# Edge features and their weight in two 12-bit halves: a pass through DRAM in layer 1's stage, and attention's edge product as two one-pass products

## What is computed

```python
# layer 1: three times, the mean over each node's incoming edges
x = segment_sum(x[src], dst) / max(counts, 1)

# layer 3: GATv2 attention, 8 heads, with 32 features on each edge
ea = concatenate([edge_attr, edge_attr.mean(0) for each node's own loop])
x_l, x_r, e = x @ W_l, x @ W_r, ea @ W_e
m = leaky_relu(x_l[src] + x_r[dst] + e, 0.2)
alpha = einsum('ehc,hc->eh', m, att)         # then softmax over each node's incoming edges
out = segment_sum(x_l[src] * a, dst)
```

## Time and profile before

| | us |
|---|---|
| median of 3 runs | 2247.66 (2246.16 to 2248.53) |
| profiled execution, first to last instruction | 2246.0 |
| PE busy in it | 1815.0 |
| DVE busy | 1330.2 |
| ACT busy | 1054.8 |
| POOL busy | 845.9 |

### The profile page before, as it was taken

One profiled execution on the slowest core, in us unless ns is written; L12 is line 12 of the kernel. 1 busy time (PEld: TensorE's weight loads), 2 busy tenths in 40 slices (PEclk: granted clock), 3 DMA queues, 4 the chain that ended last, 5 costly groups with the idle time before them and its releaser, 6 DMA issues. The chain is left out here.

```text
span 2246.0 us, 35303 instructions
## 1 busy us (share of the span) xinstructions
PE 1815.0 (81%) x10709; PEld 1262.9 (56%) x10709; DVE 1330.2 (59%) x3119; ACT 1054.8 (47%) x2333; POOL 845.9 (38%) x886
## 2 busy tenths in 40 slices
PE   5677799979999983678887888878878878888876
PEld 2567765557888851345554555545545555555554
DVE  6999967674333353755555555555545555554585
ACT  0689877645423451144434444444434344444465
POOL 1000000010000015766666666666666666666500
PEclk9555589999999997889898989998898889998887
DMA  3100000014400012323332333333322223332311
GB/s 91 40 2 1 2 8 0 0 29 124 118 1 5 3 34 74 85 75 85 80 82 75 85 81 78 82 82 83 81 78 81 81 78 85 82 80 78 79 34 29
DMA packets 132486, 133.22 MB, mean 59 GB/s; under 512 B 29049, under 2 KB 102354, under 8 KB 132306
## 3 DMA queue, kind: packets, MB, share of 16 engines
q1 hardware_dynamic: 104530, 73.76, 11.5%
q0 software_dynamic: 27776, 57.20, 10.3%
HBM read 126.05 MB, written 4.82 MB: 58 GB/s over the span
## 5 line engine op out<-in xcount | busy, mean ns | idle before, releaser
L2198 POOL DMA_INDIRECT rows<-x_l,src x856 | 821.0, 959 | 467.7 <-issue 224.7
L2323 ACT ACTIVATE bent<-psum 128x512 f32<-128x512 f32 x214 | 126.9, 594 | 532.0 <-remote 323.3
L2216 PE MATMUL psum<-hot,x_r_parts 128*128 128x256 bf16 x1284 | 205.8, 296 | 183.6 <-DVE hot L2377 97.1
L2284 PE MATMUL psum<-both,node_hot 128*128 128x144 f32 x1712 | 300.4, 318 | 56.0 <-issue 43.4
L2284 PEld LDWEIGHTS psum<-both,node_hot 128*128 128x128 f32 x1712 | 262.1, 211 | 130.3 <-issue 116.4
L2216 PEld LDWEIGHTS psum<-hot,x_r_parts 128*128 x1284 | 131.0, 102 | 342.9 <-issue 320.1
L2381 DVE TENSOR_TENSOR bent<-psum,bent 128x512 f32<-128x512 f32 x214 | 147.0, 687 | 218.8 <-ACT bent L2323 130.4
L2338 ACT ACTIVATE apart<-iota,rel 128x128 bf16<-128x128 f32 x856 | 270.5, 388 | 0.4 <-PE psum L2284 0.4
L2219 PE MATMUL psum<-edges,w_e 128*128 128x512 f32 x428 | 252.1, 671 | 10.3 <-issue 10.0
L2471 DVE TENSOR_TENSOR acc<-acc,psum 128x144 f32 x428 | 127.5, 298 | 224.1 <-remote 163.8
L2236 PE MATMUL psum<-bent,att_heads 128*128 128x512 f32 x428 | 232.0, 633 | 2.9 <-issue 1.7
(11 more groups left out here) (344 smaller groups left out, 2395.9 us busy)
## 6 DMA issues: line engine op xcount, KB each, us to landing
rel_row<-e_rel_rows SPq DMA_DIRECT2D x107, 256.0 KB
edges<-edge_t SPq DMA_DIRECT2D x428, 32.0 KB
rows<-x_l,src POOLq DMA_INDIRECT x856
edge_part<-edge_t SPq DMA_DIRECT2D x40, 320.0 KB, 3.1
new<-e_new_before SPq DMA_DIRECT2D x26, 64.0 KB
new<-e_new_behind SPq DMA_DIRECT2D x26, 64.0 KB
ht<-x SPq DMA_DIRECT2D x6, 256.0 KB, 2.8
x_l<-rows SPq DMA_DIRECT2D x4, 320.0 KB
```

Source lines behind the costliest of these rows:

```text
L2198: e.indirect_dma_start(rows[:, g % ring, j * ROW:(j + 1) * ROW], None, k.xl, bass.IndirectOffsetOnAxis(ap=src[:, at:at + 1], axis=0)).then ...
L2216: e.matmul(z[:, half], row_parts.parts[:, bass.ds(blocks[j], 1), q, :].rearrange("p o f -> p (o f)"), hot[:, two, half], start=j + q == 0, ...
L2284: final = e.matmul(to, near_hot[:, at, j, :], both[:, at, j, :], start=j % 2 == 0, stop=j % 2 == 1)
```

## The change

The edge features and `W_e` are each split into an upper half, which is the number rounded to the type `float32r`, and a lower half, which is the rest; the sum of the two is exact. A `float32r` operand goes through TensorE in one pass.

**In layer 1's stage** ACT's copy writes the upper half to a place of its own (the tile `hs`, which layer 1's last slots need later), POOL subtracts it from the piece, and SP stores both to two new DRAM tables, `edge_upper` and `edge_lower`. Pieces are 2 quads instead of 5, so there are 101 instead of 41, in 5 buffers (`edge_part`) and 4 (upper halves). ACT sums three pieces in each of the slots 0 to 33.

**In attention** SP loads four pieces in place of two for each group, the upper halves into rows 0 to 31 and the lower ones into rows 32 to 63 of `edges`. `w_e` has two matrices, each with the same half of the weight in both row ranges, so two products give all four combinations of halves.

```diff
-    share = -(-s.quads // (2 * s.nb))
-    cuts = [(c, c * share, min((c + 1) * share, s.quads)) for c in range(2 * s.nb) if c * share < s.quads]
+    share, pieces, highs = 2, 5, 4
+    cuts = [(c, c * share, min((c + 1) * share, s.quads)) for c in range(-(-s.quads // share))]
+    a_slot = -(-len(cuts) // (2 * s.nb))
...
             # layer1, gpsimd
+                for c, lo, hi in cuts:
+                    e.wait_ge(part_summed.sem, part_summed.at(c + 1))
+                    piece = piece_of(c, lo, hi)
+                    e.tensor_tensor(piece, piece, upper_of(c, lo, hi), ALU.subtract).then_inc(*part_split.up())
...
             # layer1, sync
+                def load(c, lo, hi):
+                    if c >= pieces:
+                        e.wait_ge(lower_stored[c % pieces].sem, lower_stored[c % pieces].at(16 * (c // pieces)))
+                    e.dma_start(piece_of(c, lo, hi), by_row[:, lo:hi, :]).then_inc(*part_here[c % pieces].up(16))
+
+                def store(c, lo, hi):
+                    e.wait_ge(part_split.sem, part_split.at(c + 1))
+                    e.dma_start(parts_by_row[0][:, lo:hi, :], upper_of(c, lo, hi)).then_inc(*upper_stored[c % highs].up(16))
+                    e.dma_start(parts_by_row[1][:, lo:hi, :], piece_of(c, lo, hi)).then_inc(*lower_stored[c % pieces].up(16))
+                for c, lo, hi in cuts[:pieces - 1]:
+                    load(c, lo, hi)
                 for c, lo, hi in cuts:
-                    if c >= 2:
-                        e.wait_ge(part_summed.sem, part_summed.at(c - 1))
-                    e.dma_start(part[:, c % 2, 0:hi - lo, :], by_row[:, lo:hi, :]).then_inc(*part_here[c % 2].up(16))
+                    store(c, lo, hi)
+                    if c + pieces - 1 < len(cuts):
+                        load(*cuts[c + pieces - 1])
+                for stored in upper_stored + lower_stored:
+                    e.wait_ge(stored.sem, stored.at(stored.n))
...
             # layer1, scalar, in slot q
-                        if q < len(cuts):
-                            c, lo, hi = cuts[q]
-                            e.wait_ge(part_here[c % 2].sem, part_here[c % 2].at(16 * (c // 2 + 1)))
-                            piece = part[:, c % 2, 0:hi - lo, :]
-                            e.activation(piece, piece, ACT.Copy, accum_out=sums[:, c:c + 1]).then_inc(*part_summed.up())
+                        for c, lo, hi in cuts[a_slot * q:a_slot * (q + 1)]:
+                            e.wait_ge(part_here[c % pieces].sem, part_here[c % pieces].at(16 * (c // pieces + 1)))
+                            if c >= highs:
+                                e.wait_ge(upper_stored[c % highs].sem, upper_stored[c % highs].at(16 * (c // highs)))
+                            e.activation(upper_of(c, lo, hi).bitcast(F32R), piece_of(c, lo, hi), ACT.Copy,
+                                         accum_out=sums[:, c:c + 1]).then_inc(*part_summed.up())
...
             # attention, sync, fetch(g)
-                    for j, at in enumerate(two):
-                        e.dma_start(edges[0:DE, g % edge_slots, j * 2 * P:(j + 1) * 2 * P].rearrange("d (t e) -> d t e", t=2),
-                                    rows_of_pair(at)).then_inc(*edge_here[g % edge_slots].up(16))
+                    for j, q in itertools.product(range(2), range(2)):
+                        e.dma_start(here_of[q * DE:(q + 1) * DE, g % edge_slots, j * 2 * P:(j + 1) * 2 * P].rearrange(
+                            "d (t e) -> d t e", t=2), rows_of_pair(q, two[j])).then_inc(*edge_here[g % edge_slots].up(16))
...
             # attention, tensor, begin(g)
-                    e.matmul(z, w_e[:, :], edges[:, g % edge_slots, :], start=False, stop=False).then_inc(*products.up())
+                    for q in range(2):
+                        final = e.matmul(z, w_e[:, q, :], edges[:, g % edge_slots, :], start=False, stop=False)
+                    final.then_inc(*products.up())
```

More of the change, by code:

```diff
@@ L1 @@
+import itertools
 from contextlib import ExitStack
@@ L6 @@
 F32 = mybir.dt.float32
+F32R = mybir.dt.float32r
 F16 = mybir.dt.float16
@@ L1356, in layer1 @@
     s = k.s
-    share = -(-s.quads // (2 * s.nb))
-    cuts = [(c, c * share, min((c + 1) * share, s.quads)) for c in range(2 * s.nb) if c * share < s.quads]
+    share, pieces, highs = 2, 5, 4
+    cuts = [(c, c * share, min((c + 1) * share, s.quads)) for c in range(-(-s.quads // share))]
+    a_slot = -(-len(cuts) // (2 * s.nb))
+    k.edge_parts = [k.dram(q, (s.quads, 4 * DE, P)) for q in ("edge_upper", "edge_lower")]
+    parts_by_row = [q.rearrange("i r e -> r i e") for q in k.edge_parts]
     groups = BlockGroups(s).all
@@ L1367, in layer1 @@
         tmp = sb("tmp", [P, 4, 2, D])
-        part, sums = sb("edge_part", [P, 2, share, P]), sb("edge_sums", [P, len(cuts)])
+        part, sums = sb("edge_part", [P, pieces, share, P]), sb("edge_sums", [P, len(cuts)])
+        upper = rows[:, :, :, :].rearrange("p a b e -> p (a b) e")
         v = k.flag("means_vector")
@@ L1374, in layer1, with piece_of, upper_of @@
             "moments", "roots", "factors", "rows_done", "high_next", "low_next"))
-        part_here, part_summed = [k.flag("part_here") for _ in range(2)], k.flag("part_summed")
+        part_here, part_summed = [k.flag("part_here") for _ in range(pieces)], k.flag("part_summed")
+        part_split = k.flag("part_split")
+        upper_stored = [k.flag("upper_stored") for _ in range(highs)]
+        lower_stored = [k.flag("lower_stored") for _ in range(pieces)]
+        assert highs * share == 2 * TOGETHER
+        def piece_of(c, lo, hi):
+            return part[:, c % pieces, 0:hi - lo, :]
+        def upper_of(c, lo, hi):
+            return upper[:, c % highs * share:c % highs * share + hi - lo, :]
         def await_sums(e, q):
@@ L1421, in norm_rows @@
                                 e.wait_ge(cut.sem, cut.at(g - 1))
+                            if g == 0:
+                                for stored in upper_stored:
+                                    e.wait_ge(stored.sem, stored.at(stored.n))
                             for b in range(lo, hi):
@@ L1952, in _ @@
                     if b == 4:
-                        e.tensor_copy(w_e[0:DE, :], raw[0:DE, 2, :]).then_inc(*v.up())
+                        whole, upper, lower = raw[0:2 * DE, 2, :], w_e[0:2 * DE, 0, :], w_e[0:2 * DE, 1, :]
+                        e.tensor_copy(upper, whole).then_inc(*v.up())
+                        t = v.n
+                        e.wait_ge(v.sem, v.at(t))
+                        e.tensor_tensor(lower, whole, upper.bitcast(F32), ALU.subtract).then_inc(*v.up())
         k.stage_over()
@@ L2148, in _, with rows_of_pair @@
                 pair = Registers(k, ENGINE.SP, regs[0:1, 0, :], 2 * groups, s.pairs)
[L2149 to L2152 removed]
+                pairs_t = [q.rearrange("q (v r) e -> (q v) r e", v=2) for q in k.edge_parts]
+                here_of = edges[:, :, :].bitcast(F32)
+                def rows_of_pair(q, at):
+                    return pairs_t[q][bass.ds(at, 1), :, :].rearrange("o (t d) e -> d (o t) e", t=2)
                 def fetch(g):
```

10 lines of the change are left out of this document (5 added, 5 removed).

## The result

The changed kernel takes 2344.14 us (median, 2337.06 to 2360.10) beside 2248.10: the ratio is 1.044, interval 1.0418 to 1.0461, 96 us slower. That is above the forecast's 2267 and above the range of 2205 to 2330.

What follows compares the result with a forecast made beforehand. Prediction: PE paces layer 1; in attention neither PE nor POOL fills the time, and POOL pauses for late-seen joins. 2246.0 + 70 (layer 1) - 51 (attention) = 2265 profiled, 2267 as median; range 2205 to 2330.

Steps and rivals of the forecast that it cites:

- Layer 1, +70: Layer 1: hop 1 starts at 644.0 instead of 573.47, as slots wait for the store loop; +52 to +99.
- T = 1.67: Layer 1's store loop: steady time in us per piece of 2 quads, (2.3 landing + 1.04 issues and waits)/2.
- The lower end of 1.41: Layer 1: lower bound of T, three issues of 0.46 us and two waits on SP's queue; +52 us.
- The product's price: Attention: two one-pass products take 0.44 us, one fp32 0.87; saves 0.48 with the clock, 102 us over 214.
- I take half of PE's saving, -51: Attention: half of PE's 102 us comes back, between 39 and 72 from longer gather runs; bounds 0 and -102.
- POOL's lateness as 5 us: Attention: the join of group 105 is done at 1505.95, POOL's gather starts at 1510.95, so POOL learns 5 us late.
- Hidden, so 0: Attention, SP and DMA: two more issues, 0.83 us, and 64 KB more a group cost nothing.
- the second rival's 2214: PE's whole saving comes back in attention: 2247.7 - 102 + 68 = 2214; chance 0.22.
- the forecast's own range: 2225 to 2300: layer 1 loses 52 to 99, attention gives back 25 to 75; chance 0.50.
- Attention gives nothing: Rival: 2247.7 + 70 = 2318, as `float32r` isn't one pass at bf16's rate or the clock falls; chance 0.18.
- at most +10: Attention's loads: 10 us if waits for `rel_row` grew by their whole 1.7 us in one of 20 pairs.
- 0.85 stood in the last part as the sign of it: Attention: a clock at 0.85 instead of near 0.90 would show the attention forecast wrong in size.

Runs made afterwards that it cites:

- layer1_only: Kernel before with only layer 1's split and stores added, attention as before, stored halves not read: 1.0332 of the kernel before, +75 us.
- three_ahead: Kernel with layer 1's split alone, edge loads three pieces ahead instead of four, on the 2042 us chip: 1.0373 of the kernel before, +76 us.
- product_only: Kernel before with two one-pass products in attention and single loads from a plain copy of the features: 0.9995 of the kernel before.
- no_product: Kernel before with attention's edge product left out and the loads kept, on a 2290 us chip: 0.9845 of the kernel before, -35 us.

## Why the prediction was wrong

- **Layer 1, +70: right.** Measured are 71.5 us at hop 1, 75 by layer1_only. The step "T = 1.67" was right in size for the wrong reason: it took half of a landing and its issues; three_ahead took the landing out and the round stayed, and the rows show three issues of 0.52 us, a few long ones and short holes. The lower end of 1.41 had the likelier reason, with issues 0.06 us too quick and nothing for the long ones.
- **The product's price.** Forecast: 0.43 us saved at full clock. By the medians over 214 products, from the first start to the next work, it went from 0.954 to 0.643 us; the sum from 232 to 162, 70 us and not 102 less. A float32r product is one record of 497 ns with its end, where an fp32 one is two of 671. Two of them take 0.55 to 0.64 us and not the 0.44 that bf16's rate gave: the row of another type was no measure for it.
- **"I take half of PE's saving, -51": the step that failed.** It supposed that a join 0.43 us earlier is in time for POOL's next turn, so that a pause comes after 2.3 groups and not 1.8. In the kernel after there are 122 pauses over 1 us, one for 1.75 groups. product_only gives 0.0, no_product 35 us for over three times the saving. In the traces the saving goes two ways: PE's other work at the lower clock takes some 54 of 76 us, idle time the rest. Which leads is not settled: no run changed the clock alone or the late sight alone on one chip. The prediction also read POOL's lateness as 5 us. POOL was still at its gathers for the first 3 of them and waited 2.04.
- **"Hidden, so 0": failed on the first chip.** The doubled loads cost 25 us there and 8 on another. SP's fetch of a group grew from 0.84 to 2.0 us (medians), 1.2 more where the forecast had 0.83, yet the last load of a group is issued 10.6 us (median) before its product, and from group 20 on never less than 5.7. What costs is open: the order on SP's queue isn't decided, and transfers beside the gathers are not shown.
- **The sum with what was measured.** With 0 for -51 the sum is 2318, still inside the range; with 25 for the loads' 0 it is 2343, outside it, and 2344.14 was measured. The failed saving moved the forecast, and the loads carried it over the edge. Two slips didn't matter: the second rival's 2214 has +68 where layer 1 is +70, and 99 less 25 would make the upper end of the forecast's own range 2322, not 2300.
- **The rivals.** "Attention gives nothing", 2318 at 0.18, was the nearest. Of its two mechanisms float32r's explains a part, since 32 of the 102 us were never saved, and the clock's was right in direction: 0.85 stood in the last part as the sign of it, and 0.84 was measured. No rival had attention lose; the loads stood at 0, with at most +10, and the 26 us above 2318 were missed there.

## What to carry to other kernels

Price a saving by what waits for it. Here PE was 81% busy and the joins were late, but most of the saving was not passed on to those who needed them. A kernel that leaves the whole suspected work out bounds in one step what any cut of it can give. In a loop of small DMAs on one queue, price the issues as well as the landing: here three issues took 0.52 us each with their waits, and a loop without the landing was no faster. And the chip on which a ratio was measured belongs to it: this one is 1.044 on one and 1.031 on another.

## What the runs showed of the hardware

- Five chips at least ran the same kernel before in 2042, 2248 and (three of them) 2290 us. On the 2042 us chip ACT follows a PE join by 0.04 us; on the others up to 7 us passes, often until 1 to 2 us after POOL's last gather of a run (some 80 of 109 late ones in the kernel before lie in a pause of POOL). Gathers (a median of 947 ns) and landings (2.2 us in layer 1) take the same time on both kinds. Why the chips differ no view shows.
- PE's granted clock went against its work. Over whole executions on one chip it was 0.81 without the product, 0.86 with it and 0.89 with two; in most of attention it was 0.90 before on the 2248 us chip, and 0.99 on the 2042 us chip, where late sight and POOL's pauses are absent.
- An fp32 to float32r copy on ACT runs at the rate of fp32 to fp32: 0.417 us for 256 columns, 0.406 for the smallest piece of the earlier trace rows.
